# Layer stage: the high part of the gelu values times both parts of the second matrix as one 512-column product

## The chip, the cores and the metric

The program runs on one core of a Trainium2 chip (trn2). The metric is the device time of one execution in microseconds (us). The engines are TensorE (PE, with its weight loads as PEld), VectorE (DVE), ScalarE (ACT), GpSimd (POOL) and SyncE (SP, here the engine that issues most DMAs).

## What is computed

A graph attention layer over 6250 nodes of 256 values and 100000 edges, followed by a small feed-forward net on every node, and then a top-2 mixture of eight experts. The change touches the feed-forward net of the first part:

```python
out = layer_norm(out, ln2_g, ln2_b)
ff = gelu_tanh(out @ ffn_w1 + ffn_b1) @ ffn_w2 + ffn_b2      # 256 -> 1024 -> 256
return out + ff
```

and, by the way its matrices are stored, the experts:

```python
h = gelu(einsum('end,edh->enh', xe, W1) + b1)                # eight experts, 256 -> 1024 -> 256
y = einsum('enh,ehd->end', h, W2) + b2
```

## The kernel before

Products in these two nets are made from split values. A float32 value is rounded to a high part, and the rest, full minus high, is the low part; a product is high times low, plus low times high, plus high times high, all summed in PSUM. `split_product` (L1147 to L1150) issues these three matmuls, each with a weight load of its own for the stationary operand.

There are four stages, one after the other: nodes, edges (to about 1240 us), the layer stage (about 1280 to 1638 us), and the experts (from about 1660 us).

In the edge stage the weights of the layer's net and of the eight experts are split in 72 pieces of 128 x 512 values: SP loads a piece, ACT rounds it, DVE makes the low part, and SP stores both parts in DRAM (`split_w`, L723 to L728), the high parts and the low parts of a matrix apart, one row of 8 KB a partition. Half of the pieces belong to a first matrix and half to a second one.

The layer stage goes through 49 tiles of 128 nodes in 13 batches: batches 0 to 10 have four tiles, batch 11 three, batch 12 two. The order of each engine is written out by hand, with semaphores between the engines. For a batch b:

- PE makes eight hidden blocks (`hid_product`, m = 0 to 7, six matmuls each; moving operand 512 columns) in three PSUM banks, so that block 3 needs the bank of block 0 back from ACT. Between blocks 5 and 6 it transposes rows of batch b - 1 (L1421).
- ACT turns each block by gelu into a full and a high copy (`gelus`, L1257 and L1258), and DVE makes the low part (L1144).
- PE transposes batch b + 1 (L1408), makes the gate logits of batch b - 1 (L1430), and then the output of tile j = 0 to 3 (`out_product`), 24 matmuls with the 256 columns of the second matrix as moving operand. The tiles use banks 4 and 5 in turn, so that tile 2 waits until DVE has read tile 0. Ahead of tile 3 it counts places in the experts for batch b - 1 (L1441, L1444), which needs `both` from DVE (L1568).
- DVE adds the output of each tile to the rows, `add_ff` (L1532), between the gate work of batch b - 1. Its order in this part is: three long operations of `base` (L1513, L1514, L1516), low parts of batch b + 1, start of the gates, `add_ff` 0, gates, `add_ff` 1, gates (with L1568), `add_ff` 2, statistics of tiles 0 to 2 (to L1499), the scale L1505 after POOL has taken the root (L1332), `add_ff` 3.
- ACT waits for L1505, normalizes tiles 0 to 2 (L1267), and only then takes the gelu of the next batch's block 0: both stand in that order in its program.

The expert stage runs 56 slots of 256 rows, with 48 hidden and 48 output matmuls of 256 columns a slot. Its matrices come from `split_w` by SP (L1704, L1706), each only when the expert changes.

Of the kernel before, what the change touches and what calls it, by code (L numbers as in the profile page):

```python
# [20 lines left out]
def build(nc, x, src, dst, gW, att_src, att_dst, g_bias, gW_res, ln1_g, ln1_b, ln2_g, ln2_b,  # L21
# [31 lines left out]
    with ctx:  # L53
# [33 lines left out]
        split_w = dram("split_w", [E + 1, 2, 2, P, WSZ])  # L87
# [143 lines left out]
        fw2_hi, fw2_lo = [cut(layer_w2, i * MC * D, MC, D) for i in range(2)]  # L231
# [42 lines left out]
        w2_hi, w2_lo = [[cut(eround, at + i * WSZ, MC, D) for at in (3 * BUF, 2 * BUF)] for i in range(2)]  # L274
# [448 lines left out]
        def store_piece(i):  # L723
            e, which, q = piece_at(i)
            sp.wait_ge(piece_high, i + 1)
            sp.dma_start(split_w[e, which, 0, :, q * PIECE:(q + 1) * PIECE], piece_hi[i % 2][:, :].bitcast(F32)).then_inc(piece_stored[i % 2], 16)
            sp.wait_ge(piece_low, i + 1)
            sp.dma_start(split_w[e, which, 1, :, q * PIECE:(q + 1) * PIECE], piece_lo[i % 2][:, :].bitcast(F32)).then_inc(piece_stored[i % 2], 16)  # L728
# [422 lines left out]

        def x1_stored(eng, b):
            eng.wait_ge(x1_written[b % 2], 16 * (b // 2 + 1))


        def layer_sp():
            pieces_stored(sp, N_PIECES)
            sp.wait_ge(summed, GS * (NG - 3))
            for i, to in enumerate((fw1_hi, fw1_lo)):
                sp.dma_start(to.rearrange("p a b -> p (a b)").bitcast(F32), split_w[E, 0, i, :, :]).then_inc(w1_loaded, 16)  # L1160
# [30 lines left out]
        def load_first(which, sems):  # L1191
            for part_, to in enumerate((w1_hi, w1_lo) if which == 0 else (w2_hi, w2_lo)):
                sp.dma_start(to[0].rearrange("p a b -> p (a b)").bitcast(F32), split_w[0, which, part_, :, :]).then_inc(sems[0], 16)
# [177 lines left out]
        def hid_product(b, m):  # L1371
            n, at = batch_tiles(b), MC * b + m
            if m == 0:
                pe.wait_ge(out_split, KC * b + KC)
                pe.wait_ge(w1_loaded, 32)
            bk = HID_BANK[m % 3]
            prev = at - 3 if m >= 3 else MC * (b - 1) + max(q for q in range(MC) if q % 3 == m % 3)
            if prev >= 0:
                pe.wait_ge(hid_ready, prev + 1)
            for k in range(KC):  # L1380
                ins = split_product(bank[bk][:, 0:n * P], [w[:, k, m * P:(m + 1) * P] for w in (fw1_hi, fw1_lo)],
                                    [a[b % 2][:, k, 0:n * P] for a in (out_hi, out_lo)], k == 0, k == KC - 1)
            ins.then_inc(hid_made, 1)

        def out_product(b, j):
            w, o_ = tiles_before(b) + j, bank[4 + j % 2][:, 0:D]
            if w == 0:
                pe.wait_ge(w2_loaded, 32)
# [59 lines left out]
        def layer_dve_program():  # L1448
# [77 lines left out]
            def add_ff(b, j):  # L1526
# [155 lines left out]
        def experts_sp():  # L1682
# [16 lines left out]
            def load_w(j, which, sems):  # L1699
                for part, to in enumerate((w1_hi, w1_lo) if which == 0 else (w2_hi, w2_lo)):  # L1700
                    flat = to[j % 2].rearrange("p a b -> p (a b)").bitcast(F32)
                    from_ = split_w[bass.ds(expert[j], 1), which, part, :, :].rearrange("o p c -> (o p) c")
                    if j != 1:
                        sp.dma_start(flat, from_, cond=changed[j]).then_inc(sems[j % 2], 16)  # L1704
                    else:
                        sp.dma_start(flat, from_).then_inc(sems[j % 2], 16)  # L1706

            def load_w1(j):
                if j == 0:
                    sp.wait_ge(ew1[0], 32)  # L1710
# [4 lines left out]
            def load_w2(j):  # L1715
                if j == 0:
                    sp.wait_ge(ew2[0], 32)
# [169 lines left out]
        def experts_pe():  # L1887
            layer_ended(pe)
            for j in range(NS + 3):
                jf, js = j - 2, j - 3  # L1890
                if 0 <= jf < NS:
                    i = jf % 2
                    pe.wait_ge(slot_low, jf + 1)
                    pe.wait_ge(ew1[i], 32 * (jf // 2 + (2 if i == 0 else 1)))
# [8 lines left out]
                if js >= 0:  # L1903
                    i = js % 2
                    pe.wait_ge(ehid_low_done, (MC // 2) * (js + 1))
                    pe.wait_ge(ew2[i], 32 * (js // 2 + (2 if i == 0 else 1)))
                    for t in range(2):
                        if js >= 1:
                            pe.wait_ge(y_read, 2 * (js - 1) + t + 1)
                        for m in range(MC):  # L1910
                            ins = split_product(bank[5 + t][:, 0:D], [h[i][:, m, t * P:(t + 1) * P] for h in (ehid_hi, ehid_lo)],
                                                [w[i][:, m, :] for w in (w2_hi, w2_lo)], m == 0, m == MC - 1)
# [66 lines left out]
```

## Time and profile before

| | us |
|---|---|
| median of 3 runs | 2321.96 |
| lowest, highest | 2321.76, 2322.27 |
| span of the profiled execution | 2320.4 |
| edge stage, DVE busy of 1080 | 1018.70 |
| layer stage, batches 2 to 9 (eight full batches) | 218.37 |
| expert stage, 1676 to 2310, PE busy of 634 | 634.00 |

The span is that of the one execution that was profiled, from its first to its last instruction; no time of its own beside the span is listed for it. The median of the runs stands 1.6 us above the span. Times inside the trace are given from the start of the span. In the profile a matmul's length is its latency, not its share of the engine: matmuls overlap, and what each takes is read from the distance between starts.

### The profile page before, as it was taken

Reading aid. Unit: us, or ns where it says so; the run is one execution under the profiler, and the core shown is the slowest. Engines: PE = TensorE matmul, PEld = TensorE weight load, DVE = VectorE, ACT = ScalarE, POOL = GpSimd, SP = SyncE. Lnnn points to the kernel's source line nnn. Section 1 sums busy time; section 2 is a strip of 40 time slices with the busy share of each in tenths; the row PEclk is TensorE's granted clock in tenths of the full one; section 3 lists DMA queues with packets and bytes.
Section 4 is the critical chain, followed back from the end, with each engine's and each line's share of the span. In section 5 each row is a group of like instructions: output and inputs, shape, how many; then the busy total and the mean of one; then the engine's idle time right before and its main releaser. Section 6 shows DMA issues by size and latency. Waiting matters only on the chain.

```text
span 2320.4 us, 42218 instructions
## 1 busy us (share of the span) xinstructions
PE 1770.4 (76%) x12098; PEld 1555.3 (67%) x12098; DVE 1758.3 (76%) x5422; ACT 1553.2 (67%) x3225; POOL 1183.1 (51%) x1167
## 2 busy tenths in 40 slices
PE   6526666666666666666665899999399999999998
PEld 4415444555444555444544788889399999999998
DVE  7449999999999999999999788887455555555554
ACT  3366767777666677666773687787366666666665
POOL 3277777777777777777760134445222222222223
PEclk9857777777777777777777899999699999999999
DMA  7767776777776777776663223322735356436432
GB/s 229 192 190 213 214 212 202 203 208 212 215 219 198 201 208 210 226 203 199 195 189 125 67 93 99 97 81 85 240 48 120 47 120 156 84 48 156 83 48 38
DMA packets 276602, 358.02 MB, mean 154 GB/s; under 512 B 118917, under 2 KB 208862, under 8 KB 271634
## 3 DMA queue, kind: packets, MB, share of 16 engines
q1 hardware_dynamic: 211954, 202.64, 28.0%
q0 software_dynamic: 63840, 151.61, 27.2%
q8 instruction: 97, 1.59, 0.3%
q10 hardware_dynamic: 576, 1.09, 0.2%
q14 instruction: 135, 1.11, 0.2%
HBM read 464.93 MB, written 95.79 MB: 242 GB/s over the span
## 4 chain that ended last, share of the span: by engine, by line
PE 59%; DVE 25%; issue 7%; ACT 3%; POOL 2%; DMA 2%; DVEq 1%; SPq 0%; ACTq 0%; POOLq 0%
PE bank L953 16%; PE bank L1148 12%; PE bank L1150 12%; PE bank L1149 12%; DVE edge_mem L1022 3%; PE bank L831 2%; DVE edge_sum L1066 2%; DVE win_mem L1047 2%; POOL edge_mem L765 2%; DVE piece_lo L1144 2%; DVE seg_max L1058 1%; PE bank L832 1%; PE bank L940 1%; DVE layer_rounded L1144 1%; PE bank L522 1%
## 5 line engine op out<-in xcount | busy, mean ns | idle before, releaser
L765 POOL DMA_INDIRECT edge_mem<-node_table,src_col x880 | 839.9, 954 | 281.5 <-issue 256.2
L953 PE MATMUL bank<-edge_mem 128*128 128x264 f32 x1760 | 527.0, 462 | 7.2 <-ACT edge_mem L894 4.3
L1148 PE MATMUL bank<-expert_rounded 128*128 128x256 f32 x1792 | 509.4, 284 | 27.7 <-DVE expert_rounded L1144 27.7
L1149 PE MATMUL bank<-expert_rounded 128*128 128x256 f32 x1792 | 509.0, 284 | 0.0
L1150 PE MATMUL bank<-expert_rounded 128*128 128x256 f32 x1792 | 509.0, 284 | 0.0
L953 PEld LDWEIGHTS bank<-edge_mem 128*128 128x128 f32 x1760 | 386.1, 226 | 105.1 <-issue 24.0
L1883 POOL DMA_INDIRECT out<-expert_mem,slot_tok x112 | 174.2, 1555 | 500.1 <-DVE expert_mem L1820 480.0
L1148 PEld LDWEIGHTS bank<-expert_rounded 128*128 128x128 f32 x1792 | 343.4, 192 | 28.1 <-issue 25.5
L1144 DVE TENSOR_TENSOR expert_rounded<-expert_mem,expert_rounded 128x512 fp32r<-128x512 f32 x280 | 194.0, 693 | 216.2 <-ACT expert_rounded L1870 143.2
L1870 ACT ACTIVATE expert_mem<-bank,par 128x256 f32<-128x256 f32 x448 | 221.9, 495 | 198.2 <-PE bank L1150 198.2
L1149 PEld LDWEIGHTS bank<-expert_rounded 128*128 128x128 f32 x1792 | 343.4, 192 | 0.0
L1150 PEld LDWEIGHTS bank<-expert_rounded 128*128 128x128 f32 x1792 | 343.3, 192 | 0.0
L1022 DVE TENSOR_TENSOR edge_mem<-edge_mem,bank 128x1056 f32<-128x1056 f32 x385 | 294.1, 776 | 13.9 <-ACT bank L886 13.9
L859 ACT ACTIVATE edge_mem<-iota,dst_col 128x128 bf16<-128x128 bf16 x880 | 262.8, 387 | 0.0
L1870 ACT ACTIVATE expert_rounded<-bank,par 128x256 fp32r<-128x256 f32 x448 | 222.0, 496 | 0.0
L1047 DVE TENSOR_TENSOR win_mem<-win_mem,bank 128x264 f32 x440 | 187.4, 426 | 15.3 <-PE bank L953 14.8
L1043 DVE TENSOR_TENSOR win_mem<-win_mem,bank 128x264 f32 x440 | 186.8, 425 | 2.8 <-issue 0.3
L940 PE MATMUL bank<-cand,edge_mem 128*128 128x27 bf16 x880 | 32.3, 186 | 185.9 <-DVE cand L1083 182.4
L940 PEld LDWEIGHTS bank<-cand,edge_mem 128*128 128x128 bf16 x880 | 28.1, 104 | 194.5 <-issue 194.5
L879 ACT CAST cand<-bank 128x128 bf16<-128x128 f32 x55 | 15.9, 289 | 211.2 <-PE bank L928 211.2
L922 PE MATMUL bank<-parts,edge_mem 128*128 128x48 bf16 x880 | 32.6, 186 | 148.0 <-DVE parts L1014 148.0
L922 PEld LDWEIGHTS bank<-parts,edge_mem 128*128 128x128 bf16 x880 | 26.4, 97 | 162.9 <-DVE parts L1014 162.9
(236 smaller groups left out, 3796.5 us busy)
## 6 DMA issues: line engine op xcount, KB each, us to landing
expert_rounded<-split_w SPq DMA_DIRECT2D x228, 1024.0 KB
edge_mem<-step_place SPq DMA_DIRECT2D x55, 512.0 KB, 7.3
split_w<-piece_hi SPq DMA_DIRECT2D x72, 256.0 KB
split_w<-piece_lo SPq DMA_DIRECT2D x72, 256.0 KB
piece_full<-in_L_ffn_W SPq DMA_DIRECT2D x64, 256.0 KB
expert_mem<-expert_rows SPq DMA_DIRECT2D x224, 64.0 KB, 2.8
edge_mem<-node_table,src_col POOLq DMA_INDIRECT x880
node_table<-win_mem SPq DMA_DIRECT2D x12, 544.0 KB, 4.5
```

Source lines behind the costliest of these rows:

```text
L765: pool.indirect_dma_start(gath[g % NGB][:, t, :], None, node_table, bass.IndirectOffsetOnAxis(ap=src_col[:, k, t % 2:t % 2 + 1], axis=0)). ...
L859: ins = act.activation(o16[:, t, :], iota16[:, :], ACT.Abs, scale=-1.0, bias=dst_col[:, k, t % 2:t % 2 + 1])
L953: ins = pe.matmul(bank[4 + at % 3][:, 0:AGG], onehot[g % 2][:, 2 * k + j, :], gath[g % NGB][:, 2 * k + j, 0:AGG], start=(j == 0), stop=(j ...
L1022: dve.tensor_tensor(rows_, rows_, wgt[:, r, :].unsqueeze(3).to_broadcast([P, end - first_, HEADS, HC]), ALU.mult).then_inc(weighted, 1)
L1043: t_scaled = step(dve.tensor_tensor(acc_h, acc_h, scale[:, k, :].unsqueeze(2).to_broadcast([P, HEADS, HC]), ALU.mult))
L1047: dve.tensor_tensor(acc, acc, bank[4 + at % 3][:, 0:AGG], ALU.add).then_inc(added, 1)
L1144: return eng.tensor_tensor(lo, full, hi.bitcast(F32), ALU.subtract)
L1148: pe.matmul(out_ap, s_hi, m_lo, start=start, stop=False)
L1149: pe.matmul(out_ap, s_lo, m_hi, start=False, stop=False)
L1150: return pe.matmul(out_ap, s_hi, m_hi, start=False, stop=stop)
L1870: ins = act.activation(d, bank[1 + m % 4][:, 0:SLOT], ACT.Gelu, bias=par[jf % 3][:, 2 * KC + m:2 * KC + m + 1])
L1883: pool.indirect_dma_start(out, bass.IndirectOffsetOnAxis(ap=slot_tok[:, js % NTB, t:t + 1], axis=0), yout[js % 3][:, t, :], None, compute_ ...
```

## The change

In the layer stage the output product of a tile is no longer made by `split_product` but by a new function `wide_product`. The two parts of the second matrix lie side by side for each of the eight blocks of rows, so that the high part of the gelu values, loaded once, is multiplied with both in one matmul of 512 columns, which fills the PSUM bank: columns 0 to 255 get high times high, columns 256 to 511 high times low. The low part of the gelu values times the high part of the matrix goes into columns 0 to 255 as before. A tile has 16 matmuls and 16 weight loads in place of 24 and 24. DVE adds both halves of the bank to the rows, the second after the first has ended.

For this the parts are stored in another order: of a second matrix high and low alternate every 256 columns, so the stores of its pieces are 128 x 2 x 256 in place of 128 x 512. Each matrix is loaded by one DMA of 16 KB a partition in place of two of 8 KB, in the layer and in the expert stage, and the semaphores count 16 for it in place of 32. The matmuls of the experts stay as they are.

```diff
-        split_w = dram("split_w", [E + 1, 2, 2, P, WSZ])
+        split_w = dram("split_w", [E + 1, 2, P, 2 * WSZ])
...
-        fw2_hi, fw2_lo = [cut(layer_w2, i * MC * D, MC, D) for i in range(2)]
+        fw2 = cut(layer_w2, 0, MC, 2, D)
...
+        def piece_to(e, which, q, part_, piece):
+            flat = piece[:, :].bitcast(F32)
+            if which == 0:
+                return split_w[e, 0, :, part_ * WSZ + q * PIECE:part_ * WSZ + (q + 1) * PIECE], flat
+            whole = PIECE // D
+            return (split_w[e, 1, :, :].rearrange("p (m s d) -> p m s d", s=2, d=D)[:, q * whole:(q + 1) * whole, part_, :],
+                    flat.rearrange("p (m d) -> p m d", d=D))
...
+        def wide_product(out_ap, stationary, moving, start, stop):
+            s_hi, s_lo = stationary
+            n = moving.shape[-1]
+            both_, high = moving.rearrange("p s n -> p (s n)"), moving[:, 0, :]
+            if start:
+                pe.matmul(out_ap, s_hi, both_, start=True, stop=False)
+                return pe.matmul(out_ap[:, 0:n], s_lo, high, start=False, stop=stop)
+            pe.matmul(out_ap[:, 0:n], s_lo, high, start=False, stop=False)
+            return pe.matmul(out_ap, s_hi, both_, start=False, stop=stop)
...
-            for i, to in enumerate((fw2_hi, fw2_lo)):
-                sp.dma_start(to.rearrange("p a b -> p (a b)").bitcast(F32), split_w[E, 1, i, :, :]).then_inc(w2_loaded, 16)
+            sp.dma_start(layer_w2[:, 0:2 * WSZ].bitcast(F32), split_w[E, 1, :, :]).then_inc(w2_loaded, 16)
...
-                ins = split_product(o_, [h[:, m, j * P:(j + 1) * P] for h in (hid_hi, hid_lo)],
-                                    [w_[:, m, :] for w_ in (fw2_hi, fw2_lo)], m == 0, m == MC - 1)
+                ins = wide_product(o_, [h[:, m, j * P:(j + 1) * P] for h in (hid_hi, hid_lo)],
+                                   fw2[:, m, :, :], m == 0, m == MC - 1)
...
+                v(dve.tensor_tensor(r, r, bank[4 + j % 2][:, D:2 * D], ALU.add))
                 dve.tensor_tensor(r, r, bank[4 + j % 2][:, 0:D], ALU.add).then_inc(x1_ready, 1)
```

On PE, the first output tile of batch 0 begins so before (`layer_w` is the second matrix, `layer_hid` the high and `layer_rounded` the low part of the gelu values):

```order
L1408 MATMUL bank<-ident,layer_mem 128x128 x8
L1148 MATMUL bank<-layer_w,layer_hid 128x256
L1149 MATMUL bank<-layer_w,layer_rounded 128x256
L1150 MATMUL bank<-layer_w,layer_hid 128x256
L1148 MATMUL bank<-layer_w,layer_hid 128x256
L1149 MATMUL bank<-layer_w,layer_rounded 128x256
L1150 MATMUL bank<-layer_w,layer_hid 128x256
```

and so at the same place in the changed program, where line numbers are those of the new file:

```order
L1424 MATMUL bank<-ident,layer_mem 128x128 x8
L1166 MATMUL bank<-layer_w,layer_hid 128x512
L1167 MATMUL bank<-layer_w,layer_rounded 128x256
L1168 MATMUL bank<-layer_w,layer_rounded 128x256
L1169 MATMUL bank<-layer_w,layer_hid 128x512
```

Three matmuls of 256 columns for each of the eight blocks have become one of 512 and one of 256. On DVE, batch 1 has these rows before, from the start of the gates of batch 0 (`prob`) to the addition of tile 1:

```order
L1538 TENSOR_TENSOR prob<-bank,br_b 128x32
L1541 TENSOR_REDUCE tok<-prob 128x4
L1542 TENSOR_TENSOR prob<-prob,tok 128x32
L1532 TENSOR_TENSOR layer_mem<-layer_mem,bank 128x256
L1548 TENSOR_REDUCE tok<-prob 128x4
L1549 RECIPROCAL tok<-tok 128x4
L1550 TENSOR_TENSOR prob<-prob,tok 128x32
L1552 MAX top<-prob 128x8 x4
L1555 MAX_INDEX idx<-top,prob 128x8 x4
L1532 TENSOR_TENSOR layer_mem<-layer_mem,bank 128x256
```

and these in the changed program:

```order
L1555 TENSOR_TENSOR prob<-bank,br_b 128x32
L1558 TENSOR_REDUCE tok<-prob 128x4
L1559 TENSOR_TENSOR prob<-prob,tok 128x32
L1548 TENSOR_TENSOR layer_mem<-layer_mem,bank 128x256
L1549 TENSOR_TENSOR layer_mem<-layer_mem,bank 128x256
L1565 TENSOR_REDUCE tok<-prob 128x4
L1566 RECIPROCAL tok<-tok 128x4
L1567 TENSOR_TENSOR prob<-prob,tok 128x32
L1569 MAX top<-prob 128x8 x4
L1572 MAX_INDEX idx<-top,prob 128x8 x4
L1548 TENSOR_TENSOR layer_mem<-layer_mem,bank 128x256
L1549 TENSOR_TENSOR layer_mem<-layer_mem,bank 128x256
```

Each addition of a tile has become two, at the same places; nothing else has moved on DVE.

## Rows read from the trace of the kernel before

**Rows 1.** The page: span, busy time of each engine, DMA packets.

```profile
span 2320.4 us, 42218 instructions
...
PE 1770.4 (76%) x12098; PEld 1555.3 (67%) x12098; DVE 1758.3 (76%) x5422; ACT 1553.2 (67%) x3225; POOL 1183.1 (51%) x1167
...
DMA packets 276602, 358.02 MB, mean 154 GB/s; under 512 B 118917, under 2 KB 208862, under 8 KB 271634
...
```

**Rows 2.** Three stages: length; PE, PEld, DVE, ACT, POOL busy; clock; DMA share; GB/s.

```profile
...
150.00:1230.00 1080.00, 685.74 (x3869) 522.98 (x3870) 1018.70 (x3330) 767.48 (x1447) 801.49 (x840) 0.75 0.71 207
1340.90:1559.27 218.37, 215.66 (x1523) 195.43 (x1521) 184.04 (x598) 175.54 (x303) 93.27 (x89) 1.00 0.29 94
1676.00:2310.00 634.00, 634.00 (x5283) 633.88 (x5283) 319.77 (x705) 431.55 (x1090) 169.53 (x109) 1.00 0.43 87
...
```

**Rows 3.** Timeline of PE, 1410 to 1431 us: start, length, line, [idle before <-releaser].

```profile
...
1410.81 0.28 PE L1148 MATMUL bank<-layer_w,layer_hid 128*128 128x256 f32 x1
...
1416.09 0.28 PE L1150 MATMUL bank<-layer_w,layer_hid 128*128 128x256 f32 x1
1416.65 0.39 PE L1148 MATMUL bank<-layer_w,layer_hid 128*128 128x256 f32 x1 [0.29 <-DVE layer_mem L1532]
...
1419.64 0.18 PE L1441 MATMUL bank<-both,tri 128*128 128x8 bf16 x1
...
1420.00 0.36 PE L1148 MATMUL bank<-layer_w,layer_hid 128*128 128x256 f32 x1
...
1422.95 0.40 PE L1148 MATMUL bank<-layer_rounded,layer_w 128*128 128x512 f32 x1
...
1427.07 0.40 PE L1148 MATMUL bank<-layer_rounded,layer_w 128*128 128x512 f32 x1
...
1430.93 0.39 PE L1150 MATMUL bank<-layer_rounded,layer_w 128*128 128x512 f32 x1
...
```

**Rows 4.** Timeline of DVE, 1410 to 1428 us, same batch.

```profile
...
1410.71 1.22 DVE L1513 TENSOR_TENSOR layer_mem<-layer_mem,layer_in 128x1024 f32<-128x1024 f32 x1
1411.96 1.23 DVE L1514 TENSOR_TENSOR layer_mem<-layer_mem 128x1024 f32<-128x1024 f32 x1
...
1416.19 0.41 DVE L1532 TENSOR_TENSOR layer_mem<-layer_mem,bank 128x256 f32<-128x256 f32 x1
...
1419.11 0.19 DVE L1568 TENSOR_TENSOR both<-sel 128x32 bf16<-128x32 f32 x1
...
1420.29 0.42 DVE L1532 TENSOR_TENSOR layer_mem<-layer_mem,bank 128x256 f32<-128x256 f32 x1
...
1422.28 0.16 DVE L1499 TENSOR_SCALAR z_arg<-mv 128x3 f32<-128x3 f32 x1
1423.92 0.17 DVE L1505 SCALAR_TENSOR_TENSOR z_nm<-mv,z_rs 128x6 f32<-128x6 f32 x1 [1.48 <-POOL z_rs L1332]
...
```

**Rows 5.** Timeline of ACT, 1424 to 1427 us.

```profile
...
1424.12 1.59 ACT L1267 ACTIVATE layer_mem<-layer_mem,z_nm,z_rs 128x256 f32<-128x256 f32 x3 [2.13 <-DVE z_nm L1505]
...
1426.18 0.67 ACT L1258 ACTIVATE layer_hid<-bank,fb 128x512 fp32r<-128x512 f32 x1
...
```

**Rows 6.** Waits of the eight full batches, 1340.90 to 1559.27 us.

```profile
...
DVE layer_rounded L1144 <- ACT layer_hid L1258: 13.9, 33, 0.7
...
PEld bank L1148 <- DVE layer_mem L1532: 3.5, 7, 0.5
...
```

**Rows 7.** Timeline of DVE at batches 0, 11 and 12: additions that wait for PE.

```profile
1310.86 0.42 DVE L1532 TENSOR_TENSOR layer_mem<-layer_mem,bank 128x256 f32<-128x256 f32 x1 [2.90 <-PE bank L1150]
...
1605.42 0.42 DVE L1532 TENSOR_TENSOR layer_mem<-layer_mem,bank 128x256 f32<-128x256 f32 x1 [0.34 <-PE bank L1150]
...
1624.13 0.42 DVE L1532 TENSOR_TENSOR layer_mem<-layer_mem,bank 128x256 f32<-128x256 f32 x1 [0.65 <-PE bank L1150]
```

**Rows 8.** Timeline of PE at batch 11: start of its fourth hidden product.

```profile
1590.09 0.44 PE L1148 MATMUL bank<-layer_rounded,layer_w 128*128 128x384 f32 x1 [0.53 <-ACT layer_hid L1258]
```

**Rows 9.** Waits of the edge stage, 150 to 1230 us.

```profile
...
ACT asrc L852 <- DMA edge_mem<-node_table,src_col: 39.2, 15, 4.5
...
```

More of the change, by code:

```diff
@@ L273, in build @@
         w1_hi, w1_lo = [[cut(eround, at + i * WSZ, KC, HID) for at in (BUF, 0)] for i in range(2)]
-        w2_hi, w2_lo = [[cut(eround, at + i * WSZ, MC, D) for at in (3 * BUF, 2 * BUF)] for i in range(2)]
+        w2 = [cut(eround, at, MC, 2, D) for at in (3 * BUF, 2 * BUF)]
+        w_flat = [[cut(eround, at, 2 * WSZ) for at in ats] for ats in ((BUF, 0), (3 * BUF, 2 * BUF))]
         assert 2 * WSZ <= BUF
@@ L725, in store_piece @@
             sp.wait_ge(piece_high, i + 1)
-            sp.dma_start(split_w[e, which, 0, :, q * PIECE:(q + 1) * PIECE], piece_hi[i % 2][:, :].bitcast(F32)).then_inc(piece_stored[i % 2], 16)
+            sp.dma_start(*piece_to(e, which, q, 0, piece_hi[i % 2])).then_inc(piece_stored[i % 2], 16)
             sp.wait_ge(piece_low, i + 1)
-            sp.dma_start(split_w[e, which, 1, :, q * PIECE:(q + 1) * PIECE], piece_lo[i % 2][:, :].bitcast(F32)).then_inc(piece_stored[i % 2], 16)
+            sp.dma_start(*piece_to(e, which, q, 1, piece_lo[i % 2])).then_inc(piece_stored[i % 2], 16)
+        def piece_to(e, which, q, part_, piece):
[5 more added lines that the diff above has]
+                    flat.rearrange("p (m d) -> p m d", d=D))
         def pieces_stored(eng, upto):
@@ L1158, in layer_sp @@
             sp.wait_ge(summed, GS * (NG - 3))
-            for i, to in enumerate((fw1_hi, fw1_lo)):
-                sp.dma_start(to.rearrange("p a b -> p (a b)").bitcast(F32), split_w[E, 0, i, :, :]).then_inc(w1_loaded, 16)
+            sp.dma_start(layer_w1[:, 0:2 * WSZ].bitcast(F32), split_w[E, 0, :, :]).then_inc(w1_loaded, 16)
             sp.wait_ge(summed, GS * (NG - 2))
-            for i, to in enumerate((fw2_hi, fw2_lo)):
-                sp.dma_start(to.rearrange("p a b -> p (a b)").bitcast(F32), split_w[E, 1, i, :, :]).then_inc(w2_loaded, 16)
+            sp.dma_start(layer_w2[:, 0:2 * WSZ].bitcast(F32), split_w[E, 1, :, :]).then_inc(w2_loaded, 16)
             sp.wait_ge(summed, GS * (NG - 1))
@@ L1191, in load_first @@
         def load_first(which, sems):
-            for part_, to in enumerate((w1_hi, w1_lo) if which == 0 else (w2_hi, w2_lo)):
-                sp.dma_start(to[0].rearrange("p a b -> p (a b)").bitcast(F32), split_w[0, which, part_, :, :]).then_inc(sems[0], 16)
+            sp.dma_start(w_flat[which][0].bitcast(F32), split_w[0, which, :, :]).then_inc(sems[0], 16)
         def load_residual(b):
@@ L1385, in out_product @@
         def out_product(b, j):
-            w, o_ = tiles_before(b) + j, bank[4 + j % 2][:, 0:D]
+            w, o_ = tiles_before(b) + j, bank[4 + j % 2][:, 0:2 * D]
             if w == 0:
-                pe.wait_ge(w2_loaded, 32)
+                pe.wait_ge(w2_loaded, 16)
             if j >= 2:
@@ L1699, in load_w @@
             def load_w(j, which, sems):
[L1700 to L1706, printed above, removed]
+                to = w_flat[which][j % 2].bitcast(F32)
+                from_ = split_w[bass.ds(expert[j], 1), which, :, :].rearrange("o p c -> (o p) c")
+                if j != 1:
+                    sp.dma_start(to, from_, cond=changed[j]).then_inc(sems[j % 2], 16)
+                else:
+                    sp.dma_start(to, from_).then_inc(sems[j % 2], 16)
             def load_w1(j):
                 if j == 0:
-                    sp.wait_ge(ew1[0], 32)
+                    sp.wait_ge(ew1[0], 16)
                 if j >= 2:
@@ L1716, in load_w2 @@
                 if j == 0:
-                    sp.wait_ge(ew2[0], 32)
+                    sp.wait_ge(ew2[0], 16)
                 if j >= 2:
@@ L1911, in experts_pe @@
                             ins = split_product(bank[5 + t][:, 0:D], [h[i][:, m, t * P:(t + 1) * P] for h in (ehid_hi, ehid_lo)],
-                                                [w[i][:, m, :] for w in (w2_hi, w2_lo)], m == 0, m == MC - 1)
+                                                [w2[i][:, m, s_, :] for s_ in range(2)], m == 0, m == MC - 1)
                         ins.then_inc(y_made, 1)
```

6 lines of the change are left out of this document (3 added, 3 removed).

## The prediction

> **What bounds the kernel now.** I began with the busy times of the page [rows 1]: no engine is busy for more than 76% of the span, so no engine bounds it throughout, and the stages have to be taken one by one [rows 2]. In the experts PE is busy for all of 634 us. In the edges DVE is busy for 1018.70 of 1080 us. The change adds no compute to either. In the layer stage PE looks full too, 215.66 of 218.37 us for eight batches, or 27.30 us a batch, but that is the modelled length of overlapping matmuls; DVE is busy for 184.04.
>
> So I went through one batch in the timeline, to see what waits. PE: the 44 steps from the start at 1410.81 to that at 1416.09 are 0.120 us each. The next matmul, the first of tile 2, should have started at 1416.21 and starts at 1416.65; what it waits for is `add_ff` of tile 0 on DVE [rows 3]. That addition runs from 1416.19 and is 0.41 long, so the release takes 0.05 us [rows 4]. The waits of eight batches say the same: seven waits of PE's weight load for L1532, 3.5 us in all; and DVE, for its part, waits for ACT's high gelu values 33 times, 13.9 us [rows 6]. These waits close a ring: hidden blocks on PE, gelu on ACT, low parts and `base` on DVE, `add_ff` 0, tiles 2 and 3 on PE, hidden blocks. I call it the **tile ring**. It has no slack, and 27.3 us is its length.
>
> A second ring lies almost as tight beside it. After `add_ff` 2 at 1420.29 DVE makes statistics until 1422.44, POOL takes the root, L1505 follows at 1423.92 [rows 4], ACT normalizes from 1424.12 and then makes the first gelu block, whose high part ends at 1426.85 [rows 5]. That frees the bank in which PE starts hidden block 3, at 1427.07 [rows 3]. With 0.05 for the release the slack is 1427.07 - 1426.85 - 0.05 = 0.17 us. I call it the **statistics ring**. In batch 11 it has none: PE's block 3 there waits 0.53 us for ACT [rows 8].
>
> **The change, part by part.** *Matmuls.* The sum of columns stays 768 for each of the eight blocks of a tile; what falls away is one start. A matmul of 256 columns takes 0.120 us. One of 512 takes, over the 17 steps from 1427.07 to 1430.93, 0.227 us [rows 3]. So 0.360 becomes 0.347: 0.013 us for a block, 0.107 for a tile, 5.2 us for the 392 blocks of 49 tiles. Bounds: 0.027 for a block if the second start were free as well (0.347 less the 0.013 once more, so 10.4 us in all), and zero if the mix of lengths undid it. I take 0.013; both lengths are measured in this stage. The weight loads removed are hidden under the matmuls already.
>
> The Trainium skill says in "TensorE: Matmul & The Clock Gate", section "Back-to-back issue gap", that a warm matmul starts N / 2.4 + 2.5 ns after the one before. That would be an estimated 109 and 216 ns, below the rows' 120 and 227, and the saving only 2.5 ns a block, 1.0 us in all; the sum below would then be 0.3 us higher. The trace does not agree for these matmuls, and I keep to it.
>
> *The second addition.* It is a new 128 x 256 operation of DVE that reads PSUM, the same form as L1532: 0.41 us [rows 4]. The operation behind it waits for it; between L1513 (1410.71, 1.22 long) and L1514 (1411.96), which depend on each other in the same way, 0.03 us pass. I take 0.445 us for a tile, 21.8 us for 49 tiles. Bounds: 0.34 (if the two overlapped, as neighbours that don't wait do: 1422.28 of L1499 and its neighbours overlap by some 0.08) and 0.50 (twice the gap and a little). What matters is where it lies. Between 1410.71 and 1422.44 DVE waits for no other engine (it shows only the small gaps of dependent operations), so there is no cover: `add_ff` 0 ends 0.445 later, `add_ff` 1 and L1568 0.89, and L1499 1.335.
>
> *Tile ring, one full batch.* Tile 2 starts at 1416.65 + 0.445 = 1417.10 and takes 0.107 less than 1419.64 - 1416.65 = 2.99: PE is free at 1419.98. The count needs L1568, which ends at 1419.30 + 0.89 = 1420.19, so it starts at 1420.24 in place of 1419.64; it takes 0.36, tile 3 starts at 1420.60 in place of 1420.00 and takes 2.95 - 0.107 = 2.84. The hidden blocks start at 1423.44 in place of 1422.95: **+0.49 us a batch**. The matmuls' gain ahead of tile 2 only lengthens PE's wait.
>
> *Statistics ring.* POOL and ACT wait here for DVE [rows 4, 5], so the 1.335 us pass on: the first high gelu block ends at 1428.19 and block 3 can start at 1428.24 in place of 1427.07. On the tile ring it would be ready at 1427.56. The later one counts: **+1.17 us a batch** (1.335 less the slack of 0.17). It becomes the bound: PE has a new wait of some 0.7 us ahead of hidden block 3, and everything from there goes along, since DVE's next low parts wait for ACT. `add_ff` 3 is late by 1.8 us in all when it is done; what is late next is the low part of block 0, by 0.1 us beyond ACT, which DVE's waits for ACT take up.
>
> *The whole layer stage.* Batches 1 to 9: 9 x 1.17 = 10.5 us. Batch 10 passes on to a ring without slack [rows 8]: 1.3. Three batches are different because an addition waits for PE [rows 7]. Batch 0: tile 2 starts 0.445 later and is 0.107 shorter, `add_ff` 2 costs 0.445 more, slack 0.17: 0.6. Batch 11 (statistics of two tiles): the wait of 0.34 takes up part of the first 0.445, the second stays whole: 0.55. Batch 12: its wait of 0.65 takes up the first, PE arrives 0.21 earlier, the second stays: 0.24. Sum: 10.5 + 1.3 + 0.6 + 0.55 + 0.24 = **13.2 us**.
>
> *Stores.* The 72 stores of second matrices have twice the packets. Nothing on DVE waits for them; the wait for a DMA that shows in the edge stage is ACT's for gathered rows, 39.2 us in 15 waits [rows 9], and these come in early groups, with the DMA engines at 0.71 [rows 2]. I take 0. Upper bounds: 72 x 128 = 9216 more packets are 3.3% of 276602 [rows 1]; on the 39.2 us of waits that is 1.3 us, and on 0.71 x 1080 = 767 us of DMA time, if all of it were waited for, 25 us. I lean to the first, since the bytes stay the same. Below nothing: no reason for a gain.
>
> *Loads.* One DMA of the same bytes for two. SP saves an issue for each; the layer's matrices are loaded in the edge stage, and in the experts PE shows no gap in 634 us [rows 2], so nothing can be gained there. Between the stages it can be worth a few tenths of a us. I take 0; bounds -1 and +1, the time at which the clock comes back up there included.
>
> Against the profiled execution: 2320.4 + 13.2 = 2333.6 us of span, and with the 1.6 us by which the median lies above the span, **2335.2 us**, 0.57% slower.
>
> **The rivals.** *A, the tile ring stays the bound.* If the statistics ring had 0.7 us more slack than I read, a batch would cost 0.49: ten batches 4.9, and 0.7 for the other three, 5.6 us, so 2327.6. For it: PE's wait for L1532 is the only wait of PE in full batches. Against it: the 0.17 are read from two rows of one batch, and the period of 27.3 has room for no more. Chance 0.08.
>
> *B, PE is the bound and the addition is hidden: faster.* Then the 5.2 us come through whole: 2316.8. It decides by DVE's idle time ahead of `add_ff` 0: with 0.445 us there it would hold. DVE is idle for 34 of 218 us [rows 2], but that lies at low parts and behind L1499. The Trainium skill speaks for this one: "Perfetto Trace Analysis", section "Identifying the Most-Contended Engine", takes the share of weight loads as TensorE's measure and says to relieve the most contended engine first. The rows give PEld 195.43 against DVE's 184.04 of 218.37, so by that rule PE comes first. PE's wait for L1532 speaks against it. Chance 0.07.
>
> *C, no change*, 2318 to 2326: gain and loss cancel. It needs the two rings to lose no more than 0.4 us a batch. Chance 0.06.
>
> *D, dearer than the rings*: DVE becomes the bound and each addition counts in full, 21.8 us and 2343.8; or the doubled packets slow the gathers, in the worst case by 25 us, 2360. Against the first: DVE waits for ACT 33 times in eight batches [rows 6]; against the second, 15 waits in 1080 us [rows 9]. Chance 0.09.
>
> **How the numbers follow.** The forecast has 0.70. Its own range comes from the bounds of the addition: with 0.34 a full batch costs 0.85, ten 8.5, and the rest 2, so 2332; with 0.50 it costs 1.33, ten 13.3 and the rest 3, so 2338; and 1 us for the transition either way gives 2331 to 2339. To hold the time 8 times in 10 the range goes down to A and up to where D begins: 2327 to 2342; B, C and most of D are left out. A measurement of this kernel can tell about 0.2%, 4.6 us, from no change. Slower by more: forecast, A and D, 0.87. Within: C, 0.06. Faster: B, 0.07.
>
> **What would show it.** In a full batch: a distance of 0.347 us between blocks of an output tile; two additions (L1548, L1549 of the new file) 0.445 apart; PE's wait ahead of tile 2 near 1.1 us (0.44 now); a new wait of some 0.7 us ahead of hidden block 3, released by ACT's gelu; a period of 28.5 us; the edge stage and the experts as long as before. The prediction is wrong if block 3 does not wait, if a 512-column matmul of this operand takes other than 0.227 us, or if the edge stage's periods grow.

## The result, and the profile after

| | before | after |
|---|---|---|
| time, median | 2322.11 us (2321.76 to 2324.03, 4 runs) | 2338.95 us (2337.29 to 2339.51, 4 runs) |
| ratio, 95% interval | | 1.0075 [1.0061, 1.0088] |
| span of the profiled execution | 2320.4 us | 2338.0 us |

The change makes the kernel 0.75% slower. The forecast was 2335.2 us in a range of 2327 to 2342. The page of the kernel after, the lines that answer to [rows 1]:

```profile
span 2338.0 us, 41143 instructions
...
PE 1773.7 (76%) x11706; PEld 1534.1 (66%) x11706; DVE 1780.0 (76%) x5471; ACT 1553.4 (66%) x3225; POOL 1191.9 (51%) x1167
...
DMA packets 283221, 357.96 MB, mean 153 GB/s; under 512 B 118629, under 2 KB 227006, under 8 KB 280562
```

DVE has its 49 additions more (5422 became 5471) and 392 matmuls are gone. The stages, as in [rows 2]; the eight full batches, from hidden block 0 of batch 2 to that of batch 10, now take 229.03 us in place of 218.37:

```profile
150.00:1230.00 1080.00, 686.21 (x3864) 522.66 (x3864) 1018.32 (x3322) 765.08 (x1446) 803.41 (x840) 0.75 0.70 207
1343.92:1572.95 229.03, 216.63 (x1265) 180.13 (x1264) 197.50 (x630) 175.68 (x303) 97.83 (x88) 1.00 0.28 89
1694.00:2328.00 634.00, 634.00 (x5282) 634.00 (x5281) 319.71 (x705) 432.49 (x1090) 169.47 (x109) 1.00 0.43 87
```

PE and ACT are busy for about as long as before in these batches (216.63 us against 215.66, 175.68 against 175.54), but the stretch is 10.7 us longer: for them the added time is waiting, not work. DVE is busy for 13.5 us more. The edge stage has the same busy times and the experts are full as before. Where PE waits is in its timeline of one batch, the one that answers to [rows 3] (rows without a wait cut to the starts that are used):

```profile
1423.48 0.50 PE L1166 MATMUL bank<-layer_w,layer_hid 128*128 128x512 f32 x1 [0.93 <-DVE layer_mem L1549]
...
1427.04 0.48 PE L1166 MATMUL bank<-layer_w,layer_hid 128*128 128x512 f32 x1
...
1429.91 0.40 PE L1157 MATMUL bank<-layer_rounded,layer_w 128*128 128x512 f32 x1
...
1434.65 0.50 PE L1157 MATMUL bank<-layer_rounded,layer_w 128*128 128x512 f32 x1 [0.45 <-ACT layer_hid L1274]
```

Two waits stand there. Tile 2 (1423.48) waits for the second addition of tile 0. Hidden block 3 (1434.65) waits for ACT's gelu, which [rows 3] did not show. On DVE, for [rows 4]:

```profile
1422.56 0.41 DVE L1548 TENSOR_TENSOR layer_mem<-layer_mem,bank 128x256 f32<-128x256 f32 x1
1423.00 0.42 DVE L1549 TENSOR_TENSOR layer_mem<-layer_mem,bank 128x256 f32<-128x256 f32 x1
...
1427.57 0.42 DVE L1548 TENSOR_TENSOR layer_mem<-layer_mem,bank 128x256 f32<-128x256 f32 x1
1428.03 0.42 DVE L1549 TENSOR_TENSOR layer_mem<-layer_mem,bank 128x256 f32<-128x256 f32 x1
...
1430.02 0.16 DVE L1515 TENSOR_SCALAR z_arg<-mv 128x3 f32<-128x3 f32 x1
1431.66 0.17 DVE L1521 SCALAR_TENSOR_TENSOR z_nm<-mv,z_rs 128x6 f32<-128x6 f32 x1 [1.48 <-POOL z_rs L1348]
```

and on ACT, for [rows 5]:

```profile
1431.86 1.59 ACT L1283 ACTIVATE layer_mem<-layer_mem,z_nm,z_rs 128x256 f32<-128x256 f32 x3 [3.51 <-DVE z_nm L1521]
...
1433.93 0.67 ACT L1274 ACTIVATE layer_hid<-bank,fb 128x512 fp32r<-128x512 f32 x1
```

Read it as a chain: tile 2's addition (1427.57), its second half, statistics, POOL's root, L1521 at 1431.66, ACT's normalisation until 1433.4, the gelu that ends at 1434.60, and hidden block 3 at 1434.65. The slack of 0.17 us ahead of it is gone in all eight full batches. The period of full batches went from 27.30 to 28.63 us.

Set side by side at marks that both traces have, the span's 17.6 us come from: the edge stage's end and the start of the layer stage, 1.8; batch 0, 0.6; batches 1 to 9, 12.0 (1.33 each); batch 10, 1.4; batch 11, 1.9; batch 12 and the transition, 0.4; the experts and the end, about -0.4.

### The profile page after: what moved, and what is told of

Same layout as the page of the kernel before. It is cut to its first block, busy times and chain, and to the rows that moved or that the text cites. A ratio compares the mean times of both kernels' runs of the same rounds, so it can differ in the third digit from the quotient of the medians.

```text
span 2338.0 us, 41143 instructions
## 1 busy us (share of the span) xinstructions
PE 1773.7 (76%) x11706; PEld 1534.1 (66%) x11706; DVE 1780.0 (76%) x5471; ACT 1553.4 (66%) x3225; POOL 1191.9 (51%) x1167
## 3 DMA queue, kind: packets, MB, share of 16 engines
q0 software_dynamic: 63840, 151.61, 26.5%
## 4 chain that ended last, share of the span: by engine, by line
PE 57%; DVE 26%; issue 8%; ACT 3%; POOL 3%; DMA 1%; DVEq 1%; SPq 0%; ACTq 0%; POOLq 0%
PE bank L962 16%; PE bank L1157 10%; PE bank L1159 10%; PE bank L1158 10%; DVE edge_mem L1031 3%; PE bank L840 3%; DVE win_mem L1056 2%; DVE edge_sum L1075 2%; DVE piece_lo L1153 2%; PE bank L1169 1%; DVE seg_max L1067 1%; POOL edge_mem L774 1%; PE bank L949 1%; PE bank L841 1%; DVE win_mem L1052 1%
## 5 line engine op out<-in xcount | busy, mean ns | idle before, releaser
L1157 PE MATMUL bank<-expert_rounded 128*128 128x256 f32 x1792 | 509.2, 284 | 27.7 <-DVE expert_rounded L1153 27.7
L931 PEld LDWEIGHTS bank<-parts,edge_mem 128*128 128x128 bf16 x880 | 26.3, 97 | 162.8 <-DVE parts L1023 162.8
```

What stands on the lines that cost most here:

```text
L1157: pe.matmul(out_ap, s_hi, m_lo, start=start, stop=False)
```

## The experiments

Times are medians, with a ratio to the kernel before from runs on the same chip. "Period" is the distance of hidden block 0 over the full batches 2 to 10.

**Three parts of the change, each alone.** *e1_layout_only* keeps the new order of the second matrix, its stores and its loads, and has the old product and one addition:

```
-                ins = wide_product(o_, [h[:, m, j * P:(j + 1) * P] for h in (hid_hi, hid_lo)],
-                                   fw2[:, m, :, :], m == 0, m == MC - 1)
+                ins = split_product(o_[:, 0:D], [h[:, m, j * P:(j + 1) * P] for h in (hid_hi, hid_lo)],
+                                    [fw2[:, m, s_, :] for s_ in range(2)], m == 0, m == MC - 1)
...
-                v(dve.tensor_tensor(r, r, bank[4 + j % 2][:, D:2 * D], ALU.add))
```

> The changed kernel's storing and loading of the split matrices, but the product of before (24 matmuls a tile, one addition by DVE). Theory R (rings): the loss is DVE's second addition, so the layer stage is as before; the edge stage shows whether its 1.7 us come from the stores (then 2323.7 us) or not (2322). Rival W (wide product: the 512-column product itself costs): 2322 to 2324 as well. Rival L (layout: stores and 16 KB loads cost): 2335 to 2339.

Measured: 2323.44 us, ratio 1.0006 [0.9997, 1.0016], period 27.29. The stores with twice the packets and the joined loads cost nothing clear of noise; the interval leaves room for up to 3.7 us. In the profiled execution the layer stage begins at 1285.00 us, against 1285.88 before and 1287.65 after. That speaks against the stores as the source of the edge stage's 1.8 us, but does not rule them out: this execution was 2.9 us shorter than the median of its run. Other kernels below, with either layout, begin the stage between 1284.1 and 1289.5.

*e2_no_second_add* is the changed kernel without DVE's addition of columns 256 to 511. It leaves the product of the high gelu values with the low matrix out of the result.

```
-                v(dve.tensor_tensor(r, r, bank[4 + j % 2][:, D:2 * D], ALU.add))
```

> The changed kernel without DVE's addition of columns 256 to 511, so the high gelu values times the low part of the matrix are missing from the output. Theory R: one batch of 27.3 us gets shorter by the 0.21 us of tiles 2 and 3, at most the 0.17 us of slack of the statistics ring: 11 x 0.17 = 1.9 us less in the layer stage, so 2320 to 2322 with the edge stage's 1.7 us. Rival W: still 2333 to 2339. Rival L: likewise.

Measured: 2321.15 us, ratio 1.0001 [0.9992, 1.0011], period 27.26. TensorE's shorter product alone brings almost nothing: the distance from tile 1's last start to tile 2's first grows from 0.57 to 0.87 us, which takes up what tiles 0 and 1 gave. Of what tiles 2 and 3 gave, 0.05 us a batch is left (245.28 us against 245.72 from hidden block 3 of batch 1 to that of batch 10): the distance to tile 3, behind the counting, grows from 0.49 to 0.60, and block 3 starts only 0.06 to 0.09 us behind the end of the gelu that it needs.

*e3_extra_add_only* is the kernel before with one more addition of the same form into a spare buffer, which the real one waits for:

```
+                v(dve.tensor_tensor(spare[:, :], r, bank[4 + j % 2][:, 0:D], ALU.add))
                 dve.tensor_tensor(r, r, bank[4 + j % 2][:, 0:D], ALU.add).then_inc(x1_ready, 1)
```

> The kernel before, with one more addition for each tile on DVE (rows plus the tile's bank, into a spare tile), waited for as the second addition is in the changed kernel; 24 matmuls a tile as before. Theory R: the statistics ring does not hold the matmuls of tiles 2 and 3, so the loss is nearly that of the change in the layer stage: a batch of 28.6 to 28.7 us, about 15 us in all, 2337 us. Rivals W and L: 2322 to 2323, for DVE's addition would be hidden.

Measured: 2337.74 us, ratio 1.0068 [1.0051, 1.0084], period 28.63. From hidden block 3 of batch 1 to that of batch 10 it takes 257.64 us, the changed kernel 257.71, the kernel before 245.72. So in the full batches the second addition is the whole loss, and the shorter product gives none of it back.

**Which ring?** *e4_gelu_first* is the changed kernel with ACT's normalisation of tiles 0 to 2 behind the first gelu of the next batch. That frees the bank of block 3 early and leaves the tile ring as it is.

```
                         gelus(b, m)
+                    if m == 0 and 0 <= b - 1 < NB - 1:
+                        norm_z(b - 1, 0)
...
-                if 0 <= b < NB - 1:
-                    norm_z(b, 0)
```

> The changed kernel, with ACT taking the gelu of the next batch's hidden block 0 ahead of the normalizing of tiles 0 to 2. Theory R: hidden block 3 no longer waits for DVE's statistics, POOL's root and the normalizing; the tile ring is left with +0.5 to +0.6 us a batch: 27.9 us a batch, 8 us less than the changed kernel, about 2331 us. Rivals W and L: 2339 as the changed kernel, for the order on ACT would not matter.

Measured: 2332.44 us, ratio 1.0043 [1.0026, 1.006], period 28.12. The waits of its eight full batches name what is left: the tile ring, and 0.36 us a batch for gelus that now come behind the moved normalisation.

```profile
PEld bank L1166 <- DVE layer_mem L1549: 9.6, 8, 1.3
...
PEld bank L1157 <- ACT layer_hid L1274: 2.9, 8, 0.4
```

So the statistics ring is what binds after the change, by half a microsecond ahead of the next thing.

**The rings loosened one at a time in the kernel before.** *e5_add0_early* puts the addition of tile 0 right behind the base in DVE's order; *e6_norm_spread* puts one normalisation apiece behind the gelus of blocks 0, 1 and 2.

```
                     base(b)
+                    add_ff(b, 0)
...
-                    if j < n:
+                    if 1 <= j < n:
...
                         gelus(b, m)
+                    if 0 <= b - 1 < NB - 1 and m < z_parts(b - 1)[0][1]:
+                        norm_z_tile(b - 1, m)
```

> The kernel before, with one thing moved: the addition that evicts the feed-forward products of output tile 0 stands right behind the base's in DVE's order, ahead of the splitting of the output and the shift of the gates. Theory (two rings of buffers pass the layer stage's period from batch to batch: the ring of output tiles with the z chain, and the ring of statistics with ACT's gelu, 0.17 us behind it): the first ring is loosened by about 1.9 us, the second then binds, so at most 0.17 us a batch comes back, 1.9 us over eleven batches: 2318 to 2322 us, best 2320. Rival (one ring alone): 0.5 to 1 us a batch, until TensorE binds: 2312 to 2316. Rival (TensorE bounds the stage already): no change.

> The kernel before, with one thing moved: ACT's normalisations of output tiles 0 to 2 of a batch stand one apiece behind the gelus of hidden blocks 0, 1 and 2 of the next batch, and not together ahead of them. Theory of two rings: the statistics' ring is loosened by over 1 us, the tiles' ring still binds as before: 2320 to 2324 us, best 2322. Rival (ACT's normalisations ahead of the gelus set the period): 0.5 us a batch or more comes back, 2312 to 2317. Rival (a gelu behind an inserted normalisation comes late for TensorE): 0.3 us a batch is lost, 2325.

*e5* is a clear miss: 2333.12 us, ratio 1.0046 [1.0029, 1.0063], period 28.16. The wait ahead of tile 2 is gone (the gap is 0.12 us), but a new one stands ahead of the counting in front of tile 3, in its timelines of PE and of DVE:

```profile
1422.74 0.17 PE L1441 MATMUL bank<-both,tri 128*128 128x8 bf16 x1 [0.92 <-issue]
```

```profile
1422.38 0.26 DVE L1568 TENSOR_TENSOR both<-sel 128x32 bf16<-128x32 f32 x1
```

PE's row names no releaser, but L1568 ends at 1422.64, 0.10 us ahead of it. The counting needs L1568, which in DVE's order stands behind everything that the early addition pushed back. PE came earlier, `both` later, and the period grew. The expectation looked at the two rings and not at what queues behind the moved instruction. Of the 11.7 us by which the profiled execution is longer, 7.2 lie between hidden block 3 of batch 1 and that of batch 10 (252.88 us against 245.72), two falls of the granted clock (below) among them; 3.7 lie in batches 10 and 11, with one fall each; the layer stage began 1.8 us later; and batch 0 was 1.1 us shorter.

*e6*: 2319.43 us, ratio 0.9991 [0.9981, 1.0001], period 27.30. Block 3 starts 1.20 us behind the end of its gelu now, where it was 0.22, and the period did not move, as the theory of two rings said, since the tile ring binds. The median lies 0.6 us below the range; in the profiled execution batch 12 and what follows take 2.2 us less than before.

**Both rings loosened, on either kernel.** *e7_before_all* and *e8_after_all* take both moves, and besides count the places behind all output tiles and put the addition of tile 1 ahead of the top gates:

```
                 for j in range(n):
-                    if j == 3 and is_batch(b - 1):
-                        count_places(b - 1)
                     out_product(b, j)
...
+                if n > 2:
+                    add_ff(b, 1)
                 for j in range(max(n, 2)):
-                    if j < n:
+                    if (1 if n == 2 else 2) <= j < n:
```

> The kernel before with both rings loosened: the early addition of tile 0, the spread normalisations, the addition of tile 1 ahead of the top gates, and the counting of places behind all output tiles. Theory of two rings: neither binds and TensorE does; the wait of 0.57 us ahead of output tile 2 goes, about 0.44 us a batch comes back: 2314 to 2319 us, best 2317. Rival (DVE or ACT bounds the batch through its sum): no change.

> The changed kernel with the same four moves: one product of 512 columns with two additions, both rings loosened. Theory of two rings: the second addition no longer lies on a chain that closes on itself; the period falls from 28.63 to the larger of TensorE's sum (about 26.4, with its waits 26.9) and DVE's (24.7 busy and some 1.5 of waiting, 26.2): 2308 to 2320 us, best 2316, faster than the kernel before. Rival (DVE's added work bounds the batch by its sum): the period stays above 28, 2333 to 2339. Rival (the second addition delays the eviction's buffers of TensorE at tile 2 wherever it stands): 27.3 to 27.7, 2322 to 2328.

Measured: *e7* 2322.79 us, ratio 1.0002 [0.9993, 1.0012]; *e8* 2330.47 us, ratio 1.0036 [1.0024, 1.0049]. Both missed their ranges, 2314 to 2319 and 2308 to 2320. In e7 six of the eight full batches take 26.78 us, half a microsecond less than before, and batches 2 and 5 take 28.26. Batch 5 in the windows and in the timeline of PE:

```profile
1438.05:1441.40 3.35, 3.35 (x18) 3.35 (x17) 2.97 (x5) 1.82 (x2) 2.67 (x3) 0.50 0.26 81
```

```profile
1434.80 1.95 PE L1439 MATMUL bank<-wr_sb,layer_mem 128*128 128x8 f32 x16
...
1437.77 0.28 PE L1148 MATMUL bank<-layer_w,layer_hid 128*128 128x256 f32 x1
1438.24 0.42 PE L1148 MATMUL bank<-layer_w,layer_hid 128*128 128x256 f32 x1
1438.88 0.41 PE L1148 MATMUL bank<-layer_w,layer_hid 128*128 128x256 f32 x1
```

The granted clock is 0.50 there, the lower of its two levels (1.2 and not 2.4 GHz), and a block takes 0.64 us in place of 0.36. Ahead of it PE had the transposes and the narrow logits (L1439, 128 rows by 8 columns). From hidden block 0 of batch 0 to that of batch 12 e7 takes 319.3 us against 322.5 before; without its two falls there, 3.0 us, the gain would be twice as large. This is the profiled execution, 2320.20 us; others of e7 took up to 2326.30, and their falls are not on record. A further fall in batch 12 costs 0.8 us (17.18 us from hidden block 0 to the last output matmul, 16.38 in the next experiment), and not the 2.8 that its expectation says. The fourth stretch at half clock that it counts begins behind the layer's last output matmul, as one does in every kernel here. The kernel before has none between 1290.4 and 1628.3 us. In e8 batches without a wait or a fall take 26.3 to 26.5 us, and most take 27.7: hidden blocks 4 to 6 wait for gelus, since ACT waits 1.0 us for L1530 with the first of the spread normalisations.

**The logits parted from the transposes.** *e9_before_logits* and *e10_after_logits* are e7 and e8 with the logits behind output tile 0 in every batch.

```
-                if is_batch(b - 1) and b != NB - 1:
+                if is_batch(b - 1) and not is_batch(b):
                     logits(b - 1)
...
-                    if j == 0 and b == NB - 1:
+                    if j == 0 and is_batch(b - 1):
                         logits(b - 1)
```

> The kernel before with both rings loosened as in e7, and on TensorE the router's logits of the batch ahead moved behind output tile 0 in every batch, not only in the last. e7's trace gives 26.78 us for a batch in which the granted clock stays at full speed, and four stretches of 3.4 us at half clock (batches 2 and 5 about 1.5 us longer each, batch 12 about 2.8), each behind the transposes and logits ahead of output tile 0. Theory (short, narrow products in one unbroken stretch bring the clock down): parted by a wide output tile they no longer do, the falls go, 5 to 6 us come back: 2315 to 2319 us, best 2317. Rival (the logits feed DVE's softmax, which would come some 2.9 us later and hold the output or the counting): 27.3 us a batch or more, 2323 to 2330. Rival (the falls have to do with something else): four falls as in e7, 2322.

> The changed kernel with all moves of e8 and the logits behind output tile 0 in every batch. e8 has batches of 26.4 us where nothing waits and of 27.7 where hidden blocks 4 to 6 wait for ACT's gelus (0.1 to 0.3 us apiece), and five stretches of half clock. Theory: the falls go (6 us), the wait for the gelus stays: 2322 to 2327 us, best 2325; if the gelus come in time as well, 2312. Rival (DVE's work, moved back behind the logits, holds the next batch): 2330 to 2338.

Measured: *e9* **2313.14 us, ratio 0.9969 [0.9956, 0.9981]**, faster than both kernels and 1.9 us better than its range; *e10* 2325.31 us, ratio 1.002 [1.0011, 1.003]. Eight full batches of e9 in the windows:

```profile
1345.00:1560.00 215.00, 215.00 (x1535) 197.40 (x1534) 186.12 (x602) 178.12 (x309) 95.27 (x88) 1.00 0.30 95
```

PE is busy all the time, the clock is 1.00, and a batch takes 26.57 us. Hidden block 0 of batch 12 comes 313.4 us behind that of batch 0, 9.1 us sooner than in the kernel before. e10 still has falls, in batches 2 and 3, each behind the logits in their new place, and one in batch 12 behind a wait of PE for ACT. So parting the narrow matmuls is not by itself what prevents a fall; what decides stays open. Its batches 5 to 8 take 27.7 us, for the gelus as in e8; the other full batches without a fall take 26.2 to 27.2.

**The price of the wide product with neither ring in the way.** *e11_after_later* and *e12_before_later* are e10 and e9 with the normalisations of tiles 0 to 2 one block later, and that of tile 3 behind block 4 in place of block 2.

```
-            return (2, 5, 6) if b < NB - 1 else (3, 7, 7)
+            return (4, 5, 6) if b < NB - 1 else (3, 7, 7)
...
-                    if 0 <= b - 1 < NB - 1 and m < z_parts(b - 1)[0][1]:
-                        norm_z_tile(b - 1, m)
+                    if 0 <= b - 1 < NB - 1 and 0 <= m - 1 < z_parts(b - 1)[0][1]:
+                        norm_z_tile(b - 1, m - 1)
```

> e10 (the changed kernel with all moves) with one thing more: ACT's normalisations of output tiles 0 to 2 stand behind the gelus of blocks 1, 2 and 3, and not 0, 1 and 2, that of tile 3 behind the gelu of block 4. In e8 and e10 the first of them waits 1.0 us for the statistics, which a second addition per tile makes late, and the gelus behind it hold TensorE in hidden blocks 3 to 6 (batches of 27.7 us against 26.2 to 26.6 where nothing waits). Theory (the second addition costs where a chain behind it closes, and nothing where none does): the gelus come in time, a batch falls to 26.2 to 26.6 us, 2308 to 2318 us, best 2312. Rival (DVE's sum of work now bounds the batch): it stays at 27.2 or above, 2321 to 2327. A fall of the granted clock would add 1.5 us apiece.

> e9 (the kernel before with all moves) with the same later normalisations as e11, so that e11 has a partner with the old product of 256 columns. In e9 no gelu is waited for and a batch takes 26.57 us: theory: no change by this, 2310 to 2316 us, best 2313. Rival (a later normalisation of tile 3 holds the turning of the rows behind hidden block 5): 0.2 to 0.5 us a batch slower, 2315 to 2319. The difference of e11 to it is the price of the wide product with its second addition when neither ring binds: by TensorE's intervals (0.36 against 0.347 us for each of 32 steps a batch) 0.4 us a batch less, 4 us in all, before any wait.

Measured: *e11* 2334.17 us, ratio 1.0051 [1.0035, 1.0068]; *e12* 2327.96 us, ratio 1.0027 [1.0015, 1.004]. Both missed their times, and their rivals' too, by a wait that I had built in: the last normalisation stands behind the gelu of block 4, which PE has only just made, and the transposes behind block 5 need it. In the waits of e12's eight batches:

```profile
PEld bank L1430 <- ACT layer_mem L1278: 14.1, 8, 1.8
```

e11 has the same wait, 14.1 us in eight, so the pair still answers the question in part. The gelus come in time in both, and the period is 27.88 us in e11 and 28.09 in e12; from block 3 of batch 1 to that of batch 10 it is 250.89 against 252.86. With the additions beside it and no ring of DVE's in the way, the wide product **gives** 0.22 us a batch. That is half of what the intervals promise, 0.43 or 0.107 for a tile: from the starts of tiles 0 to 3 to what follows each, e11 is shorter by 0.01, 0.08, 0.10 and 0.06 us. In tile 0 it has a wait for DVE's low parts that e12 does not show:

```profile
PEld bank L1168 <- DVE layer_rounded L1153: 1.7, 7, 0.2
```

The rest of the shortfall was not traced. The totals go the other way for reasons outside the full batches: in the profiled executions e11's layer stage began 5.4 us later, for a reason that is not known, and it had two falls of the clock, in batches 11 and 12, where e12 had none.

## Why the prediction was right, and where its sizes were off

**The mechanism stood as written.** *Statistics ring* was to become the bound, with a new wait ahead of hidden block 3 released by ACT's gelu. It did, in all eight full batches, and e4 and e6 move the period as two rings beside each other would; e5 does not test them, since a third chain that I had not listed came in. By the distance between starts PE waits 1.10 us ahead of tile 2, as said, and 0.61 ahead of block 3, where 0.7 was said (the idle times in the rows are 0.93 and 0.45). Rival A falls with the wait at block 3, rival C with the interval of the result. One ground given for A was wrong as well: PE's wait for L1532 is not its only one in the full batches before, for its weight load also waits for ACT ahead of the logits, 2.6 us in eight, before and after alike. Rival B falls with e2 and e3: the matmuls' gain is not merely outweighed, it is all but absent while an addition releases PE. Of rival D, the 25 us of the stores fall with e1, and DVE as the bound with its 197.50 us of 229.03 and with e8, where batches with both additions take as little as 26.3 us.

**The term 1.17 us a full batch was mis-sized**; it measured 1.33, so batches 1 to 9 cost 12.0 and not 10.5. Two parts of it can be read. An addition costs 0.46 us (1427.57 to 1428.03), not 0.445, three times a batch: from the start of `base` to the end of the gelu it takes 17.52 us in place of 16.14, which gives 1.21 at block 3. The other 0.12 us lies behind the wait: PE starts again slowly (its first matmul is 0.50 long in place of 0.40, and from block 3 to block 4 it takes 1.50 us in place of 1.38), which the sum had not counted. The *tile ring*, hidden now, moved by 0.59 where 0.49 was said (from the start of `base` to hidden block 0 12.83 us in place of 12.24). The forecast's bound of 0.50 for an addition gives the same 1.33 a batch, but that is chance: no addition cost 0.50.

The layer stage and the rest of the span came out 4.4 us above the sum of 13.2. These are, rounded, 1.5 from the term above, 1.8 from the edge stage, 1.3 from batch 11, and 0.3 from batches 10 and 12, less 0.4 in the experts.

**Smaller terms.** Batch 0: 0.6 said, 0.6 measured. Batch 10: 1.3 and 1.4. Batch 12: 0.24 and 0.4. **Batch 11: 0.55 and 1.9**, for a reason that no term held: the granted clock fell. The windows of the kernel after, then its PE timeline at batch 10:

```profile
1585.69:1589.11 3.42, 3.12 (x27) 2.84 (x26) 3.05 (x8) 3.42 (x7) 1.31 (x2) 0.99 0.00 0
1589.11:1592.52 3.41, 3.41 (x12) 2.92 (x12) 3.22 (x5) 2.23 (x3) 2.80 (x3) 0.51 0.15 56
1592.52:1616.41 23.89, 22.54 (x149) 20.51 (x149) 17.05 (x67) 17.62 (x36) 15.15 (x15) 1.00 0.32 106
1616.41:1619.82 3.41, 3.41 (x12) 2.83 (x11) 2.62 (x8) 1.84 (x4) 1.71 (x2) 0.51 0.22 80
```

```profile
1586.68 1.95 PE L1446 MATMUL bank<-wr_sb,layer_mem 128*128 128x8 f32 x16 [0.30 <-ACT layer_mem L1293]
...
1589.66 0.63 PE L1169 MATMUL bank<-layer_w,layer_hid 128*128 128x512 f32 x1
1590.30 0.63 PE L1169 MATMUL bank<-layer_w,layer_hid 128*128 128x512 f32 x1
...
1593.74 0.40 PE L1169 MATMUL bank<-layer_w,layer_hid 128*128 128x512 f32 x1
1594.10 0.40 PE L1169 MATMUL bank<-layer_w,layer_hid 128*128 128x512 f32 x1
```

Both falls stand behind the logits. The first costs nothing that shows, since PE would have waited ahead of tile 2 anyhow. The second makes PE late with output tiles 0 and 1 of batch 11, and DVE's additions wait for it:

```profile
1619.49 0.42 DVE L1548 TENSOR_TENSOR layer_mem<-layer_mem,bank 128x256 f32<-128x256 f32 x1 [0.68 <-PE bank L1169]
...
1622.55 0.42 DVE L1548 TENSOR_TENSOR layer_mem<-layer_mem,bank 128x256 f32<-128x256 f32 x1 [0.56 <-PE bank L1169]
```

The sum had no such wait left in batch 11; these 1.24 us are about the 1.3 by which it missed. No run at this period has batch 11 without a fall, so this is read from a trace and not tested. e3 has the same two falls with the old product, so they do not need the wide matmul. e2, with the wide product and the period of before, has one too, in batch 10, so the pace of the batches is not shown to be the cause either.

**The edge stage** was taken at 0 and came out 1.8 us later. e1 has the same stores and does not show it in its profiled execution, but its median leaves room for it. These runs do not tell a cost of the stores from the spread between kernels, so the source stays open. The *loads* were 0 as said.

**The interval of 0.347 us** for a block is what the timeline shows where nothing waits, at the starts of L1169 in batch 11's tile 1:

```profile
1620.66 0.39 PE L1169 MATMUL bank<-layer_w,layer_hid 128*128 128x512 f32 x1
1621.01 0.39 PE L1169 MATMUL bank<-layer_w,layer_hid 128*128 128x512 f32 x1
1621.36 0.39 PE L1169 MATMUL bank<-layer_w,layer_hid 128*128 128x512 f32 x1
```

The Trainium skill's "TensorE: Matmul & The Clock Gate", section "Back-to-back issue gap", gives N / 2.4 + 2.5 ns as the gap of an isolated warm matmul; for 256 and 512 columns that would be an estimated 0.325 us together. The trace does not agree with it here.

## What to carry to other kernels

Find the ring of waits that closes on itself, and put a new operation's cost on it in full, once for every time it stands there; a gain on an engine that this ring makes wait is worth almost nothing, as e2 shows. Look for the second ring before trusting the first: here it lay 0.17 us behind, and whoever loosens one must list what queues behind the moved instruction (e5 lost 11 us). And a busy share near 100% on PE does not make it the bound, as long as a single wait stands in each batch: only with both rings loosened was PE busy throughout (e9). Even so the wide product did not pay: e8 was 7.7 us slower than e7 and e10 12.2 us slower than e9, since the second additions made the statistics and with them the gelus late, and the clock fell more often. A gain of its own, 0.22 us a batch, shows only in the full batches of e11 against e12.

## What was not expected of the hardware

The granted clock falls to 0.50 for 3.4 us in some batches and not in others that do the same work: in the profiled executions twice in the kernel after and four times in e5, and in no batch of the kernel before, e1, e6, e9 and e12 once the clock was up at about 1290 us. A fall costs 1.5 us where PE is the bound (e7), and 0.4 to 0.5 in batches 5 and 9 of e5, where PE waits otherwise ahead of tile 3. In batches 1 to 11 there are 19 falls, in nine kernels. Of these, 18 began between 0.1 us ahead of and 1.3 us behind the end of the narrow logits matmuls, wherever these stand. The other one, in batch 11 of e11, and those in batch 12 of e7, e10 and e11 lie behind waits of PE for ACT of 1.5 to 2.0 us. Why one batch falls and the next does not was not settled, and e9 and e10, which differ in the product with its additions and in the layout, show that the order of PE's work alone does not decide it.
